# Work for TensorE across a gather, halved loads, and the second layer's first tiles moved in a two-layer mixture-of-experts kernel

## The reference

```python
x = x + L0_ffn(L0_cond(x, fside, lens, ...))   # attention of 16 heads, then 24 experts, the best 2 per token
x = x + L1_ffn(L1_cond(x, ...))                # masked pooling, then 8 experts (best 2) + a shared expert
# L1_cond: scores = tanh(h @ W1 + b1) @ v; p = softmax(mask(scores)); pooled = (p @ h) / count
# L1_ffn:  y = sum over the best 2 experts of w * (silu(x@wg) * (x@wu)) @ wd   (width 176)
#          + (silu(x@sw_gate) * (x@sw_up)) @ sw_down                            (width 352)
```

## Time and profile before

| what | us |
|---|---|
| median of 3 runs | 506.56 |
| lowest and highest of them | 504.57, 507.07 |
| the profiled execution, device time | 503.64 |
| its span in the trace | 501.9 |
| PE, DVE, ACT, POOL busy | 404.4, 305.0, 237.4, 225.7 |

### The profile page before, as it was taken

How to read it: one execution, slowest core, us unless ns; L and a number is a source line. 1 busy time by engine, 2 the same in 40 slices (tenths; PEclk the granted TensorE clock), 3 DMA queues, 4 the chain that set the end, 5 groups by cost and what they waited for, 6 DMA issues and landing times.

```text
span 501.9 us, 11390 instructions
## 1 busy us (share of the span) xinstructions
PE 404.4 (81%) x2728; PEld 281.7 (56%) x2729; DVE 305.0 (61%) x1225; ACT 237.4 (47%) x702; POOL 225.7 (45%) x260
## 2 busy tenths in 40 slices
PE   3588887989999998707999999817968998999940
PEld 3344444545555554406999999702655556777730
DVE  2558899888888888742333333333565634777734
ACT  1266665666767676414555555303643222444410
POOL 3336676433333343144444444447077710666640
PEclk9999998999999999857999999965887998999985
DMA  2005998788888999946776677231011110233207
GB/s 61 10 13 136 260 245 204 192 212 224 206 207 211 255 233 245 302 128 172 188 195 173 174 180 183 73 109 59 1 48 53 54 49 22 71 87 83 78 19 247
DMA packets 58356, 71.09 MB, mean 142 GB/s; under 512 B 8738, under 2 KB 34583, under 8 KB 58192
## 3 DMA queue, kind: packets, MB, share of 16 engines
q1 hardware_dynamic: 53008, 61.15, 47.9%
q0 software_dynamic: 4736, 8.47, 5.1%
q10 hardware_dynamic: 576, 1.06, 0.7%
HBM read 35.58 MB, written 36.37 MB: 143 GB/s over the span
## 4 chain that ended last, share of the span: by engine, by line
PE 42%; DVE 5%; DMA 4%; ACT 2%; issue 2%; POOLq 0%; POOL 0%; SPq 0%; DVEq 0%; ACTq 0%
PE bank L899 9%; PE bank L893 9%; PE bank L1060 6%; PE bank L1000 2%; PE bank L1075 2%; PE bank L1076 2%; PE bank L1066 2%; PE bank L989 1%; PE bank L990 1%; PE bank L953 1%; PE bank L942 1%; PE bank L885 1%; PE bank L960 1%; PE bank L1055 1%; PE bank L938 1%
## 5 line engine op out<-in xcount | busy, mean ns | idle before, releaser
L1204 ACT ACTIVATE hT<-bank,w 128x128 f32<-128x128 f32 x176 | 50.9, 368 | 53.9 <-PE bank L893 53.6
L681 POOL DMA_INDIRECT expert_rows<-rows,slots x32 | 31.6, 986 | 93.9 <-DVE slots L1410 88.8
L762 PE MATMUL bank<-qexp 128*128 128x512 f32 x128 | 69.9, 628 | 0.8 <-POOL qexp L672 0.8
L693 POOL DMA_INDIRECT expert_outputs<-yb,idr x44 | 43.2, 983 | 54.3 <-DVE yb L1560 54.3
L771 PEld LDWEIGHTS bank<-ident,ps 128*128 128x128 f32 x256 | 28.2, 142 | 66.0 <-ACT ps L1110 36.9
L742 POOL DMA_INDIRECT layer_outputs<-w_all,idr x40 | 39.3, 983 | 42.9 <-DVE w_all L1757 24.5
L771 PE MATMUL bank<-ident,ps 128*128 128x128 f32 x256 | 41.1, 284 | 19.8 <-ACT ps L1110 13.8
L1126 ACT ACTIVATE pT<-bank 128x512 f32<-128x512 f32 x64 | 38.2, 597 | 36.5 <-PE bank L771 36.5
L1386 DVE TENSOR_REDUCE mx<-bank 128x4 f32<-128x512 f32 x64 | 44.0, 687 | 12.2 <-PE bank L762 8.3
L899 PE MATMUL bank<-w_all,hT 128*128 x352 | 49.5, 284 | 1.3 <-issue 0.6
L893 PE MATMUL bank<-xT,w 128*128 128x128 f32 x352 | 49.1, 284 | 1.0 <-DVE xT L1553 0.5
(11 more groups left out here) (289 smaller groups left out, 888.2 us busy)
## 6 DMA issues: line engine op xcount, KB each, us to landing
expert_rows<-fill SPq DMA_DIRECT2D x64, 390.0 KB, 6.0
w<-in_L_ffn_w_dram SPq DMA_DIRECT2D x40, 258.0 KB, 2.8
w_all<-in_L_ffn_w_dram SPq DMA_DIRECT2D x24, 256.0 KB, 5.6
xt<-expert_rows SPq DMA_DIRECT2D x45, 65.0 KB, 3.0
w_all<-expert_rows SPq DMA_DIRECT2D x40, 65.0 KB, 1.8
qexp<-expert_outputs SPq DMA_DIRECT2D x4, 512.0 KB, 3.9
qexp<-layer_outputs SPq DMA_DIRECT2D x4, 512.0 KB, 5.5
aux<-in_L_ffn_b_dram SPq DMA_DIRECT2D x1, 1536.0 KB
```

Source lines behind the costliest of these rows:

```text
L681: g.indirect_dma_start(xs0_dram, bass.IndirectOffsetOnAxis(ap=slots[p][:, k:k + 1], axis=0), rows[k][:, i - 6, :], None).then_inc(scattere ...
L693: g.indirect_dma_start(ys_dram, bass.IndirectOffsetOnAxis(ap=idr[r][:, 0:1], axis=0), yb[r][:, :], None, bounds_check=YS1 - 1, oob_is_err= ...
L762: pe.matmul(psA[j % 2][:, :], qexp[p][:, j, :], kexp[p].rearrange("p g k -> p (g k)"), start=True, stop=True).then_inc(a_in_ps, 1)
L1204: s.activation(hT[r % 2][:, c, :], banks[c][:, 0:P], ACT.Gelu, bias=w1[r][:, F0 + c:F0 + c + 1]).then_inc(gelu_done, 1)
```

## The change

It has five edits.

- **Unread matmuls.** After the last `down`, PE issues 12 matmuls of `ident` with 128x512 of `poolbias` into bank 0 (`ps_rows`). Nothing reads their result; `pooled_rows(0)` overwrites it.
- **Halved first load.** SP loads only sequences 0 and 1 of block 0. ACT, after its last Gelu, runs one Exp of one column, waits for the same four `y_out` semaphores and loads sequences 2 and 3 (`gathered_half`). DVE mixes the halves one after the other.
- **POOL behind DVE.** POOL's `mixing(1)` waits for `x2_first`, raised when DVE has mixed block 0.
- **`logits(0)` ahead of `inner(2)`** in PE's order.
- **First tiles and last third.** `shared(3, 2)` moves behind `turn_tile1(0)` and `turn_tile1(1)` on PE and behind `turned1(0)` and `turned1(1)` on DVE. `up1(0)` waits for 11 thirds instead of 12. So that the tiles don't meet banks 2, 3 and 6, the second layer's steps get the banks (0, 1), (7, 5), (4, 2) and (6, 3), and the row of `rem1` goes to bank 1.

Further, `gate1`'s transposition uses a second count of `table_in_ps` instead of a semaphore of its own.

```diff
@@ -370,6 +370,8 @@
 
         pair = [(banks[6], banks[4]), (banks[7], banks[5]), (banks[2], banks[3])]
         ps_rows, ps_acc = banks[0], banks[6]
+        turn1, both1 = (banks[0], banks[1]), (banks[7], banks[5])
+        hidden_T1, down_1 = (banks[4], banks[2]), (banks[6], banks[3])
 
         psT = banks[0:2]
         psA = banks[2:4]
@@ -399,6 +401,7 @@
         CHAIN_TYPES = 13
         STEPS = B + 6
         LEAD = 8
+        UNREAD = 12
         LOADS = 6
 
         def pipeline(eng, step):
@@ -544,7 +547,8 @@
             ys_b = ys_dram.rearrange("(b t k) d -> t b k d", t=P, k=2)
 
             def load_block(k):
-                sp.dma_start(yv[k % 2], ys_b[:, BLK * k:BLK * (k + 1), :, :]).then_inc(gathered[k % 2], 16)
+                n = BLK // 2 if k == 0 else BLK
+                sp.dma_start(yv[k % 2][:, 0:n, :, :], ys_b[:, BLK * k:BLK * k + n, :, :]).then_inc(gathered[k % 2], 16)
 
             for r in ring:
                 sp.wait_ge(y_out[r], nl * 16 + 16)
@@ -719,6 +723,7 @@
 
             pool.wait_ge(gT_ready, 1)
             pool.wait_ge(x_added, 1)
+            pool.wait_ge(x2_first, 1)
             for k in range(1, NB):
                 mixing(k)
 
...
@@ -1000,9 +1005,11 @@
                         y = pe.matmul(ps_acc[:, t * P:(t + 1) * P], hsh[c][0:m, t * P:(t + 1) * P], wsd[0:m, c, :], start=(c == 0), stop=(c == NS1 - 1))
                 y.then_inc(out_acc, 1)
 
+            pe.wait_ge(pool_const, ALL_CONSTS)
+            for _ in range(UNREAD):
+                pe.matmul(ps_rows[:, :], ident[:, :], poolbias[:, 0:BLK, :].rearrange("p b l -> p (b l)"), start=True, stop=True)
             pe.wait_ge(gT_ready, 1)
             pe.wait_ge(y_ready, nl * RING + RING)
-            pe.wait_ge(pool_const, ALL_CONSTS)
             for k in range(2):
                 turn_x2(k)
                 inner(k)
@@ -1011,8 +1018,8 @@
             turn_x2(2)
             pooled(0)
             pooled_rows(0)
+            logits(0)
             inner(2)
-            logits(0)
             score(2)
             turn_x2(3)
             turn_pn(1)
@@ -1040,7 +1047,8 @@
                 shared(k, 0)
                 shared_down(k - 1)
                 shared(k, 1)
-                shared(k, 2)
+                if k < NB - 1:
+                    shared(k, 2)
 
             words = [None] * (TILES1 // 8)
 
@@ -1052,18 +1060,18 @@
             def turn_tile1(j):
                 r = j % RING1
                 pe.wait_ge(xt1_in[r], 16 * (j // RING1 + 1))
-                pe.transpose(banks[j % 2][:, 0:P], xt1[r][:, 0:P], ident[:, :]).then_inc(xT1_in_ps, 1)
+                pe.transpose(turn1[j % 2][:, 0:P], xt1[r][:, 0:P], ident[:, :]).then_inc(xT1_in_ps, 1)
 
             def up1(j):
                 e = expert(j)
                 pe.wait_ge(xT1_ready, j + 1)
-                pe.matmul(banks[2 + j % 2][:, 0:2 * F1], xT1[j % 2][:, :], wgu1[:, bass.ds(e, 1), :].rearrange("p o f -> p (o f)"),
+                pe.matmul(both1[j % 2][:, 0:2 * F1], xT1[j % 2][:, :], wgu1[:, bass.ds(e, 1), :].rearrange("p o f -> p (o f)"),
                           start=True, stop=True).then_inc(gu1_in_ps, 1)
 
             def turn_hidden1(j):
                 pe.wait_ge(ht1_ready, j + 1)
                 for c in range(2):
-                    m = pe.transpose(banks[4 + j % 2][:, c * P:(c + 1) * P], ht1[j % 2][:, c * P:(c + 1) * P], ident[:, :])
+                    m = pe.transpose(hidden_T1[j % 2][:, c * P:(c + 1) * P], ht1[j % 2][:, c * P:(c + 1) * P], ident[:, :])
                 m.then_inc(hT1_in_ps, 1)
 
             def down1(j):
...
@@ -1079,10 +1087,12 @@
             pe.wait_ge(rows_ready, NB)
             turn_tile1(0)
             turn_tile1(1)
-            pe.wait_ge(hsh_ready, NS1 * NB)
+            shared(NB - 1, NS1 - 1)
+            pe.wait_ge(hsh_ready, NS1 * NB - 1)
             up1(0)
             pe.wait_ge(plan1_ready, 2)
-            pe.matmul(banks[7][:, P:P + TILES1], ones_row[:, :], rem1[:, :], start=True, stop=True).then_inc(rem1_in_ps, 1)
+            pe.wait_ge(xT1_ready, 2)
+            pe.matmul(turn1[1][:, P:P + TILES1], ones_row[:, :], rem1[:, :], start=True, stop=True).then_inc(rem1_in_ps, 1)
             shared_down(NB - 1)
             for j in range(1, TILES1 + 2):
                 if j < TILES1:
@@ -1208,6 +1218,11 @@
             with act.Fori(1, nl + 1) as n:
                 round_of_tiles(n, False)
 
+
+            s.activation(gelu_warm[:, :], eg[:, 0:1], ACT.Exp)
+            for r in ring:
+                act.wait_ge(y_out[r], nl * 16 + 16)
+            act.dma_start(yv[0][:, BLK // 2:, :, :], ys_dram.rearrange("(b t k) d -> t b k d", t=P, k=2)[:, BLK // 2:BLK, :, :]).then_inc(gathered_half, 16)
 
             def keep_x2T(k):
                 act.wait_ge(x2T_in_ps, k + 1)
...
@@ -1585,16 +1600,18 @@
             cx.join()
             def mixing(k):
                 dve.wait_ge(x_added, 1)
-                dve.wait_ge(gathered[k % 2], 16 * (k // 2 + 1))
-                for t in range(BLK):
-                    b = BLK * k + t
-                    cx.add(v.scalar_tensor_tensor(out=mix1[:, t, :], in0=yv[k % 2][:, t, 0, :], scalar=g1[:, b:b + 1], in1=a_all[:, b, :],
-                                                  op0=ALU.mult, op1=ALU.add))
-                cx.join()
-                for t in range(BLK):
-                    b = BLK * k + t
-                    m = v.scalar_tensor_tensor(out=x2[:, b, :], in0=yv[k % 2][:, t, 1, :], scalar=g2[:, b:b + 1], in1=mix1[:, t, :],
-                                               op0=ALU.mult, op1=ALU.add)
+                for half, loaded in enumerate((gathered[k % 2], gathered_half)):
+                    dve.wait_ge(loaded, 16 * (k // 2 + 1))
+                    ts = range(half * BLK // 2, (half + 1) * BLK // 2)
+                    for t in ts:
+                        b = BLK * k + t
+                        cx.add(v.scalar_tensor_tensor(out=mix1[:, t, :], in0=yv[k % 2][:, t, 0, :], scalar=g1[:, b:b + 1], in1=a_all[:, b, :],
+                                                      op0=ALU.mult, op1=ALU.add))
+                    cx.join()
+                    for t in ts:
+                        b = BLK * k + t
+                        m = v.scalar_tensor_tensor(out=x2[:, b, :], in0=yv[k % 2][:, t, 1, :], scalar=g2[:, b:b + 1], in1=mix1[:, t, :],
+                                                   op0=ALU.mult, op1=ALU.add)
                 m.then_inc(x2_first, 1)
 
             def peak(k):
@@ -1728,7 +1745,7 @@
             unused_rows()
             shared_sum(1)
             for k in range(2, NB):
-                for c in range(NS1):
+                for c in range(NS1 if k < NB - 1 else NS1 - 1):
                     shared(k, c)
                 if k < NB - 1:
                     shared_sum(k)
...
@@ -1754,12 +1771,13 @@
                 cx.link(v.tensor_copy(number1[j % 2][:, :], xt1[r][:, P:P + 1].bitcast(U32)))
                 v.scalar_tensor_tensor(out=idr1[r][:, :], in0=number1[j % 2][:, :], scalar=float(2 * YS1 - 1), in1=unused1[:, j:j + 1],
                                        op0=ALU.min, op1=ALU.max)
-                v.tensor_scalar(yb1[r][:, :], banks[6 + j % 2][:, 0:P], xt1[r][:, P + 1:P + 2], None, ALU.mult).then_inc(yb1_ready, 1)
+                v.tensor_scalar(yb1[r][:, :], down_1[j % 2][:, 0:P], xt1[r][:, P + 1:P + 2], None, ALU.mult).then_inc(yb1_ready, 1)
 
             turned1(0)
             turned1(1)
+            shared(NB - 1, NS1 - 1)
             dve.wait_ge(rem1_in_ps, 1)
-            cx.link(v.tensor_scalar(unused1[:, :], banks[7][:, P:P + TILES1], iota_p[:, 0:1], float(YS1), ALU.is_le, ALU.mult))
+            cx.link(v.tensor_scalar(unused1[:, :], turn1[1][:, P:P + TILES1], iota_p[:, 0:1], float(YS1), ALU.is_le, ALU.mult))
             hidden1(0)
             shared_sum(NB - 1)
             for j in range(1, TILES1 + 2):
```

More of the change, by code:

```diff
@@ L259, in attention_moe_kernel @@
         cb_ready = sem("cb_ready")
-        gT_in_ps = sem("gT_in_ps")
+        gathered_half = sem("gathered_half")
         gT_ready = sem("gT_ready")
@@ L877, in _ @@
             pe.wait_ge(w_l1, 16 * 13)
-            pe.transpose(psZ[:, 0:E1], gate1[:, :], ident[0:E1, 0:E1]).then_inc(gT_in_ps, 1)
+            pe.transpose(psZ[:, 0:E1], gate1[:, :], ident[0:E1, 0:E1]).then_inc(table_in_ps, 1)
             pe.wait_ge(plan_ready, 1)
@@ L1073, in down1 @@
                     pe.wait_ge(yb1_ready, j - 1)
-                y = banks[6 + j % 2][:, 0:P]
+                y = down_1[j % 2][:, 0:P]
                 pe.matmul(y, hT1[j % 2][:, 0:P], wda1[:, bass.ds(e, 1), :].rearrange("p o d -> p (o d)"), start=True, stop=False)
@@ L1297, in _ @@
                         act.wait_ge(ht1_ready, j - 1)
-                    s.activation(sg1[j % 2][:, :], banks[2 + j % 2][:, 0:F1], ACT.Silu).then_inc(silu1_done, 1)
+                    s.activation(sg1[j % 2][:, :], both1[j % 2][:, 0:F1], ACT.Silu).then_inc(silu1_done, 1)
                 if j >= 1:
@@ L1302, in _ @@
```

(8 more changed lines are left out.)

## The result

The changed kernel ran in 500.41 us (median of 4, 498.18 to 501.12), the kernel before in 505.84 (median of 4). The ratio is 0.9886, with a 95% interval from 0.9853 to 0.9919: 4 to 7.4 us faster, against 8 forecast. The time lies inside the range, 1.8 us above the value.

What follows compares the result with a forecast made beforehand. PE bounds most of the chain, but has nothing for 11.75 us before block 0, which then runs at 1.2 GHz. 1.4 + 2.3 + 1.3 - 0.3 + 3.3 = 8.0; 506.56 - 8.0 = 498.6 us, range 494.3 to 501.5.

Steps and rivals of the forecast that it cites:

- Term 1: Start of block 0: bound by PE's unread matmuls, the first turn_x2 comes at 334.9 instead of 336.35, 1.4 us gained.
- Terms 2 and 3: Block 0's PE steps at the higher clock, 2.3 us, and Exp's table load off the chain, 1.28 us.
- the likeliest case: Clock holds until score(0) is through, then a low stretch from about 342 to 351; 498.6 us, chance 0.50.
- Term 3: Block 0's Exp table load moves behind ACT's last Gelu, off the chain: 1.28 us gained, bounds 1.28 and 0.
- POOL held back: POOL's mixing of block 1 starts later but stays covered to some 0.2: nothing lost, 0.5 us if uncovered.
- `logits(0)` ahead of `inner(2)`: Moved order on PE delays tanh(2) and score(2) by eight small matmuls: 0.3 us lost, bounds 1.0 lost and 1.0 gained.
- The middle: Block 1 to the shared expert moves as a whole: 0; 2 gained or about 1 lost if low stretches change.
- Term 4: Last third: up1(0) waits for the product before, and the clock holds in the last shared_down: 3.3 us gained.
- The sum: All terms of the whole kernel together: 8.0 us gained, 498.6 us against a median of 506.56.
- the second rival: Block 0: the clock falls when the unread matmuls end, so they buy none; 6.0 us gained, 500.6, chance 0.17.

Runs made afterwards that it cites:

- e2_no_unread: The changed kernel with 0 unread matmuls instead of 12; ratio 0.9883 to the kernel before.
- e10_no_unread: The changed kernel with 0 unread matmuls, run again in another group; ratio 0.9944 to the kernel before.
- e11_no_warm: The changed kernel without the Exp of one column behind the last Gelu; ratio 0.9894 to the kernel before.
- e5_whole_load: The changed kernel with block 0 loaded whole by SP, DVE still mixing in two halves; ratio 0.9911 to the kernel before.
- e4_logits_only: The kernel before with nothing but logits(0) moved ahead of inner(2); ratio 1.0061 to the kernel before.
- e8_after: The changed kernel itself, run again as a control in the second group; 497.29 us, ratio 0.9847 to the kernel before.
- controls: The two repeat runs of the unaltered changed kernel, e0_after and e8_after; both have ratio 0.9847 to the kernel before.
- e3_old_tail: The changed kernel with shared(3, 2) again ahead of the first tiles and the wait for 12 thirds, new banks kept; ratio 0.9881 to the kernel before.
- three groups: The twelve follow-up kernels ran in three groups, the kernel before beside each, with medians of 534.84, 506.15 and 533.42 us.
- e0_after: The changed kernel itself, run again as a control in the first group; 525.86 us, ratio 0.9847 to the kernel before.
- e7_fill: The changed kernel with inner(2) ahead of logits(0) and five more unread matmuls in blocks 0 and 1; 496.02 us, ratio 0.9796 to the kernel before.

## Why the prediction was right, and where it was off

**Term 1, the start of block 0.** Right: 1.4 forecast, 1.6 measured. The matmuls took 10.46 (forecast 10.3), DVE was done at 336.57, 0.7 us ahead of the first `turn_x2`, and PE was bound by its own unread work. e2_no_unread and e10_no_unread show that price, 0.2 to 0.4 us. The halves landed 3.3 to 3.7 and 3.8 to 4.2 us after their issue, the whole load in 3.91. The rule of the Trainium skill ("DMA: Bandwidth & Descriptors", section "Issuing engines are not separate DMA queues") that they interleave on the same engines agrees for the second half, which gained 0.1 at best; the first gained 0.2 to 0.6, more than the nothing that I drew from the rule.

**Terms 2 and 3.** Their sum was 3.6 and came as 3.4. `inner` and `score` of block 0 ran at the higher clock at 1.04 and 1.12. The clock fell in 340 to 344, as the likeliest case had it. Term 3 was over-priced: e11_no_warm puts it at 0.3 to 1.1, not 1.28. The 2.66 us that the Trainium skill ("ScalarE: Activation LUTs", section "What ACT_TABLE_LOAD costs") would give the switch is more than that run lost.

**POOL held back.** Forecast as nothing, 0.5 if uncovered. It is on the path by 0.16 us, the wait of `turn_x2(1)`, and in e5_whole_load a POOL that starts 0.3 to 0.6 later makes `turn_x2(1)` as much later. The cover was named right, and thinner than I took it.

**`logits(0)` ahead of `inner(2)`: the step that failed.** I took 0.3 lost within bounds of 1.0. The trace gives 1.0 for the order (7.8 against 6.8 us to `score(2)`), and e4_logits_only 3.1 us in whole (1.8 to 4.4) in the kernel before, beyond my bound. What I left out is that the moved order opens a wait of PE, 0.77 ahead of `score(2)`, in a stretch where the clock had just returned. I priced instructions moved, and not the idle time they open.

**The middle: 0.** Beside the 0.3 of the order it was -2.6 in the first trace, beyond my bound of 1 lost, and +0.8 in e8_after, inside it (-1.9 and +1.5 beside the 1.0 that the order came to). What differs most between these two profiles of one program is the second low stretch, which my sum had no term for. The controls' 7.7 us gained is near the 8.0, the first measurement's 5.8 is not. The mean clocks of the single executions go the same way, but only one execution of each kernel was traced, so that this stretch makes the whole difference is likely and not shown. Why the clock falls there in one execution and not in another stays open.

**Term 4.** 3.3 forecast, 3.4 measured, and its two halves apart: 1.7 of order (e3_old_tail), and a clock that no longer falls.

**The sum.** 8.0 forecast; 5.5 from the last `down` on in the first pair of profiles, 8.6 with the profile of e8_after. That the first measurement, 500.41, lies inside the range is partly luck: the range went up to 501.5 for the sake of the second rival, in which the unread matmuls buy no clock (500.6). That rival did not happen, since block 0 ran at the higher clock; the loss came in the middle, where I had put nothing.

## What to carry to other kernels

Where PE waits for a gather, matmuls that nobody reads can keep its clock. Here they ended up to 0.5 us after the data was there, and brought the end of block 0 1.4 to 2.3 us forward all the same. When a step is moved in an in-order queue, ask not only what comes later but whether the queue now stands idle behind it: moving eight small matmuls ahead of one large cost 1.0 us in the traces and 3.1 in the kernel with that edit alone. A gain of clock can be lost in the next stage, so follow it to the first stage that was at the higher clock anyway before counting it.

## What was not expected of the hardware

In two of the three groups DVE and ACT stopped together while POOL's scatters went on one after the other. In e0_after:

```profile
396.24 0.16 DVE L1706 CAST words<-wordf 1x5 int32<-1x5 f32 x1
...
403.67 0.96 POOL L737 DMA_INDIRECT expert_rows<-rows,places  x1 [0.30 <-issue]
...
407.34 0.69 DVE L1687 TENSOR_TENSOR w_all<-bank,w_all 128x512 f32<-128x512 f32 x1 [10.94 <-remote]
407.39 0.60 ACT L1274 ACTIVATE w_all<-bank 128x512 f32<-128x512 f32 x1 [14.18 <-remote]
```

DVE is idle for 10.94 us and ACT for 14.18, and the trace names no releaser of the program ("remote"). Both go on at 407.3 to 407.4, 2.7 us after the end of POOL's last scatter instruction. All eight profiles of these groups have such a stop, of 8.5 us or more on DVE, and neither the first two profiles nor the four of the second group do. In e0_after the stretch from the last `down` to the second `shared_down` is 18.5 us longer than in e8_after (89.5 against 71.0), of some 28 us between the groups' medians of before. It is not the chip alone: the second and the third group ran on the same one, without and with the stops. What causes it was not found.

The clock also fell where PE was far from idle: in e7_fill PE is busy for 2.00, 1.55 and 1.90 of 2 us in the three rows from 352 to 358, and the granted clock is 1.00, 0.95 and 0.50.
